# One program instead of two for the choice of experts, semaphores cleared inside the next norm, and fetches first: an eight-layer network on one core

## The reference, cut to what matters

```python
scores = softmax(xf @ gate_weight.T).T            # (8, 2048)
vals, idx = top_k(scores.reshape(-1), 2 * 2048)
gate = zeros((8, 2048)).at[idx // S, idx % S].add(vals)
h = gelu(einsum('sd,edf->esf', xf, W1) + b1[:, None, :])
y = einsum('esf,efd->esd', h, W2) + b2[:, None, :]
out = einsum('es,esd->sd', gate, y) + gelu(xf @ Ws1 + bs1) @ Ws2 + bs2
```

## Time and profile before

| | |
|---|---|
| median of 3 runs | 1896.82 us (1896.57 to 1897.28) |
| the profiled execution's own time | 1899.36 us |
| its span in the profile | 1897.6 us |
| PE busy | 1541.0 us (81%) |
| DVE busy | 1039.2 us (55%) |
| ACT busy | 924.2 us (49%) |
| POOL busy | 411.2 us (22%) |
| granted clock of PE, mean | 0.903 of full speed |

### The profile page before, as it was taken

The page is one execution under the profiler, slowest core; times in us unless marked ns, Lnnn a source line. Parts: engine busy times, 40 slices in busy tenths (PEclk is TensorE's granted clock), DMA queues, the critical chain, the costliest instruction groups (busy, mean ns, idle before and its releaser), DMA issues. The chain is left out here.

```text
span 1897.6 us, 22237 instructions
## 1 busy us (share of the span) xinstructions
PE 1541.0 (81%) x7296; PEld 664.5 (35%) x7296; DVE 1039.2 (55%) x2156; ACT 924.2 (49%) x1578; POOL 411.2 (22%) x370
## 2 busy tenths in 40 slices
PE   4699998899848898779799870674899977699997
PEld 1244443343302333234233430672122223344443
DVE  8577772100006999947577649423888825433332
ACT  4766665432257887520166640222477762234343
POOL 4101100000027898700022200560121100000000
PEclk7799998999958999989799985796699997899999
DMA  5112200100000000000111091013121102000000
GB/s 141 43 33 54 60 19 7 56 0 0 19 9 1 5 5 5 1 30 1 35 29 40 1 361 46 18 21 126 59 69 60 35 21 85 6 1 0 0 0 22
DMA packets 51965, 72.21 MB, mean 38 GB/s; under 512 B 11442, under 2 KB 44490, under 8 KB 50103
## 3 DMA queue, kind: packets, MB, share of 16 engines
q1 hardware_dynamic: 49814, 69.20, 12.0%
q0 software_dynamic: 2048, 1.73, 0.5%
HBM read 48.29 MB, written 18.12 MB: 35 GB/s over the span
## 5 line engine op out<-in xcount | busy, mean ns | idle before, releaser
L656 ACT ACTIVATE a_probs_sb<-a_t_ps 128x512 f32<-128x512 f32 x512 | 286.7, 596 | 129.3 <-PE a_t_ps L537 72.8
L747 DVE CUSTOM_DVE_ANT_0 a_biased<-a_s_ps,a_bias 128x512 f32<-128x512 f32 x256 | 166.2, 686 | 67.8 <-issue 67.6
L533 PE MATMUL a_t_ps<-a_stack 126*128 126x512 bf16 (+1 forms) x512 | 169.6, 395 | 30.4 <-DMA a_stack<-a_least_parts 11.7
L514 PE MATMUL a_s_ps<-a_stack 96*128 96x512 bf16 (+1 forms) x512 | 155.4, 412 | 39.4 <-DMA a_stack<-a_stacks 25.3
L1429 DVE TENSOR_TENSOR_SCAN s_h<-s_dA,s_dbu 128x1024 f32<-128x1024 f32 x64 | 146.6, 2290 | 52.9 <-POOL s_dbu L1394 44.3
L754 DVE TENSOR_REDUCE a_least_sb<-a_s_ps 128x2 f32<-128x1024 f32 x128 | 152.7, 1220 | 34.4 <-PE a_s_ps L514 34.1
L1394 POOL TENSOR_TENSOR s_dbu<-s_du,s_bs 128x1024 f32<-128x1024 f32 x64 | 152.3, 2391 | 29.5 <-DVE s_h L1429 27.9
L2843 ACT ACTIVATE c_hid<-c_up_ps,c_b 128x512 f32<-128x512 f32 x128 | 87.9, 687 | 143.6 <-PE c_up_ps L2812 143.6
L2853 DVE TENSOR_TENSOR c_gated_sb<-c_hid,c_g_ps 128x2048 f32<-128x2048 f32 x32 | 73.2, 2288 | 146.4 <-ACT c_hid L2843 146.4
L552 PE MATMUL a_o_ps<-a_probs_sb,a_vpad 128*16 128x512 f32 x1024 | 138.7, 615 | 0.2 <-ACT a_probs_sb L656 0.2
L2812 PE MATMUL c_up_ps<-xT,c_w 128*128 x256 | 118.0, 605 | 6.0 <-DMA c_select<-in_c_select 6.0
(11 more groups left out here) (452 smaller groups left out, 2539.9 us busy)
## 6 DMA issues: line engine op xcount, KB each, us to landing
x_wu<-in_x_wu SPq DMA_DIRECT2D x2, 4096.0 KB, 17.9
a_stacks<-a_p SPq DMA_DIRECT2D x16, 384.0 KB, 3.0
a_stack<-a_stacks SPq DMA_DIRECT2D x32, 192.0 KB, 3.9
a_stack<-a_stacks SPq DMA_DIRECT2D x64, 96.0 KB, 2.3
a_stacks<-a_p SPq DMA_DIRECT2D x16, 256.0 KB, 2.4
q_q<-q_q SPq DMA_DIRECT2D x32, 128.0 KB, 2.3
x_wd<-in_x_wd SPq DMA_DIRECT2D x2, 2048.0 KB, 33.5
c_w<-in_c_w SPq DMA_DIRECT2D x2, 2048.0 KB, 10.6
```

The lines of the kernel that those rows point to most:

```text
L514: made = nc.tensor.matmul(s_ps[:, 2 * (x % 2) + e, :], operand(0, k, pair, e, SCORE_ROWS)[:, t * P:(t + 1) * P], operand(1, k, pair, e, SC ...
L533: last = nc.tensor.matmul(out, operand(1, k, pair, e, TURNED_ROWS)[:, t * P:(t + 1) * P], operand(0, k, pair, e, TURNED_ROWS), start=True, ...
L656: nc.scalar.activation(probs[:, y % PROB_RING, e, :], bank("turned", y, e), ACT.Exp, scale=-1.0).then_inc(probs_ready, 1)
L747: nc.vector.tensor_tensor_reduce(out=biased[:, e, :], in0=s_ps[:, 2 * (x % 2) + e, :], in1=bias[:, h, at:at + N], scale=1.0, scalar=3.0e38 ...
```

## The change

- **Semaphores.** All semaphores are flags from zero. The nops that add one and their barriers are gone, and `core.sem` with them. The program that cleared a stage's semaphores is gone; POOL clears them (`clear_stale`) within the program of the next stage's norm.
- **Gated MLP.** The hardware loops are written out, with waits against constants; the order of the work is the same.
- **Layers 4 and 5** are one stage: the weights of layer 5 are loaded at the end of the prefetch of layer 4's norm, and the clearing between them is gone.
- **Sparse.** The ring of 8 fetched and 8 result tiles becomes one tile per expert. POOL issues all 32 fetches first (a fetch waits until the fourth before it has landed), then all 32 results. DVE makes places and weights for each group of 2 experts, 16 times, where it made them for 4 experts, 8 times. ACT and DVE run in a hardware loop over 8 turns of 2 groups, with six turns in the loop; PE's list stays written out. Ten of the semaphores are started at one by POOL within the routing program.
- **Choice.** `choice_route` and `choice_experts` are one program, `choice`. The loads of the two tables and of the bias go into the prefetch of the norm, in another order. PE makes the up products of unit 0 before the first count of the search. After the search PE makes one of the last four shared down products, then the places, then the other three, then the up products of units 1 and 2, the first transposes of the gates, the up products of unit 3, and from there, in each unit n, the spread of unit n+1, the up products of unit n+3 and the down products of unit n. The gelus of ACT run three units ahead in a ring of four; DVE writes the product with the gates in place. PSUM has three banks for up products of both kinds; two banks serve the routing. The loops over chunks are written out; the search stays a loop.

The diff, cut to its core ("..." marks what is left out):

```diff
-    def run_stage(self, stage, *args):
-        self.stage_sems = []
-        with ExitStack() as self.stage_ctx:
-            stage(self, *args)
-            with self.nc.Block() as block:
-                @block.gpsimd
-                def _(pool):
-                    for handle in self.stage_sems:
-                        pool.sem_clear(handle)
+    def clear_stale(self, pool):
+        for handle in self.stale_flags:
+            pool.sem_clear(handle)
+        self.stale_flags = []
+
+    def run_stages(self, stages, *args):
+        stale_ctx = ExitStack()
+        for stage in stages:
+            self.stage_ctx, self.stage_flags = ExitStack(), []
+            stage(self, *args)
+            stale_ctx.close()
+            stale_ctx, self.stale_flags = self.stage_ctx, self.stage_flags
...
 def layernorm_stage(core, xT, tag, out=None, prefetch=None, wide_range=False):
...
+        @block.gpsimd
+        def _(pool):
+            core.clear_stale(pool)
...
 def gated_mlp_stage(core, A, xT):
...
-            with pe.Fori(0, B - 1) as i:
+            for i in range(B - 1):
                 first(i)
                 up(i + 1)
                 second_and_out(i)
...
+def moe_and_query_stage(core, A, xT):
...
+                sp.dma_start(wg[:, :], A["m_wg"]).then_inc(w_loaded, 16)
+                sp.dma_start(wd[:, :, :], A["m_wd"]).then_inc(w_loaded, 16)
+                query.load(sp, A)
...
 def sparse_experts(...):
...
             def fetch(e):
-                if e >= X_RING:
-                    pool.wait_ge(turned, (e - X_RING) // PAIR + 1)
-                    pool.wait_ge(weighed, (e - X_RING) // SOME + 1)
+                if e >= SOME:
+                    pool.wait_ge(fetched[e % SOME], 16 * (e // SOME))
...
-            for e in range(X_RING):
+            for e in range(E):
                 fetch(e)
             for e in range(E):
-                if e + X_RING < E:
-                    fetch(e + X_RING)
                 scatter(e)
...
-def choice_route(core, xT, M, wr, tri, ones, ones_b, bits, unit, loaded, shared_loaded):
+def choice(core, xT, W, loaded, shared_loaded, first_loaded, w_loaded, out):
...
             last.then_inc(logits_ready, 1)
+            wait(pe, first_loaded, 32)
+            up(0)
+            wait(pe, shared_loaded, 48)
+            for i in range(B):
+                for m in range(CH_HT):
+                    count_all(CH_HT * i + m)
+                    shared_up(i, m)
+                    if i > 0:
+                        shared_down(i - 1, m)
             count_all(SEARCH_STEPS)
-            for m in range(CH_HT):
-                down(B - 1, m)
-            pe.wait_ge(equal_ready, START + 1)
+            shared_down(B - 1, 0)
+            wait(pe, equal_ready, 1)
             for n, summed in enumerate((tri, ones)):
                 last = nc.tensor.matmul(places_ps[:, n, :, :], ...)
             last.then_inc(places_ready, 1)
...
+            for m in range(1, CH_HT):
+                shared_down(B - 1, m)
+            wait(pe, w_loaded, 64)
+            for n in range(1, AHEAD):
+                up(n)
+            turn_gates(0)
+            up(AHEAD)
+            spread_gates(0)
+            turn_gates(1)
+            turn_gates(2)
+            for n in range(UNITS):
+                if n + 1 < UNITS:
+                    spread_gates(n + 1)
+                if n > 0 and n + AHEAD < UNITS:
+                    up(n + AHEAD)
+                if n == 1:
+                    turn_gates(3)
+                down(n)
...
+            def gate(n):
+                mine = hid[:, n % HID_RING, :, :]
+                wait(dve, spread_ready, n + 1)
+                wait(dve, gelu_ready, CH_HT * (n + 1))
+                nc.vector.tensor_tensor(mine, mine, g_ps[n % 2][:, :]..., ALU.mult).then_inc(gated_ready, 1)
```

More of the change, by code:

```diff
@@ L1015, in _ @@
             gate(0)
-            with dve.Fori(0, B - 1) as i:
+            for i in range(B - 1):
                 gate(i + 1)
@@ L1947, in sparse_stage @@
     results_zeroed = core.flag("x_results_zeroed")
+    counted = [core.flag(name) for name in COUNTED]
     with ExitStack() as mem:
@@ new lines, in experts @@
+            def experts(i):
+                for u in range(UNITS):
+                    up(i, u)
+                    if u == 0:
+                        turn(i, 1)
+                    if u == PAIR + 1 and not (isinstance(i, int) and i == TURNS - 1):
+                        turn(i + 1, 0)
+                    if u > 0:
+                        down(i, u - 1)
+                    elif not (isinstance(i, int) and i == 0):
+                        down(i - 1, UNITS - 1)
+            turn(0, 0)
@@ L2413, in _ @@
+            pe.wait_ge(w_loaded, 16 * 8)
+            for i in range(TURNS):
+                experts(i)
+            down(TURNS - 1, UNITS - 1)
             for i in range(B):
@@ L2490, in _ @@
+            keep(0, 0)
+            run(dve, experts)
             for i in range(B):
@@ new lines, in down @@
+            def down(n):
+                i, e = divmod(n, E)
+                wait(pe, gated_ready, n + 1)
+                if n == 0:
+                    wait(pe, y_copied, B)
+                if e == 0:
+                    wait(pe, added, i)
+                for k in range(CH_HT):
+                    last = nc.tensor.matmul(y_ps[:, :], w2[:, e, k, :], hid[:, n % HID_RING, k, :],
+                                            start=(e == 0 and k == 0), stop=(e == E - 1 and k == CH_HT - 1))
+                    if e == 0 and k == 0:
+                        nc.tensor.matmul(y_ps[:, :], b2[:, :], gates[:, cols(i)], start=False, stop=False)
+                last.then_inc(down_ready, 1)
@@ L3069, in network @@
         core.load_more_x = load_more_x
-        zeroed = core.sem("ident_zeroed")
+        zeroed = core.flag("ident_zeroed")
         with core.block() as block:
```

805 lines of the change are left out of this document (394 added, 411 removed).

## The result

The changed kernel takes 1826.98 us (median of 4 runs, 1825.61 to 1828.27) against 1897.05 (1896.57 to 1897.42): a ratio of 0.963, with an interval of 0.961 to 0.965. The forecast was 1842.8 with a range of 1834 to 1853. The sign was right and the gain too small: 72.8 us between the two spans (1897.6 and 1824.8), where 54.0 were forecast. By the medians it is 70.1 us: the profiled execution of the kernel before lies over its median, that of the changed kernel (1826.66 us) at it.

The account below looks back on a forecast made before the run. PE, busy for 1541 of 1897.6 us, was taken as the bound, so gains come from its idle or slow-clock stretches. Terms 29.9 + 0 + 4.3 + 17.3 + 2.5 = 54.0 us off 1896.8 gave 1842.8, range 1834 to 1853.

Parts of the forecast that it names:

- 1. Clearing: Entrances to programs: clearing of semaphores leaves the path, PE waits less; 29.9 us gain, bounds 26 and 31.
- Rival A: Entrances cost what they do for reasons other than clearing; if half of 23.3 us stays, 1854.5; chance 0.05.
- 2. Gated MLP: Gated MLP and layer 4: loops written out in the same order, and the prefetch, gain 0; bounds -1 and +1.
- 3. Fetches: Sparse experts: all fetches first, POOL remains the bound; 4.3 us gain, bounds 0 and 5.
- 4. Layer 8: Experts start while gates are made: 20.2 less a 1.4 wait and 1.5 for the search, 17.3 us; bounds 12 and 20.
- the head of the search: Layer 8: moving unit 0's up products before the first count delays the search, price 1.5 us.
- C: Layer 8's overlap pays half: search waits cost 6.4 us, DVE-bound sparse stage 3 us more; 1852; chance 0.12.
- D: Slower: PE is starved of instructions in layer 8's written-out units; 1908; chance 0.03.
- 5. The clock: Norms before layers 4, 8 and the last keep more clock after shorter waits; 2.5 us gain, bounds 0 and 11.
- The interpolation between two norms: Norms before layers 4 (clock 0.77) and 8 (0.86) set the gains: 1.1, 0.7 and 0.7 us for three norms.
- Rival B: Every norm keeps the full clock: six norms give 11.2 us instead of 2.5; 1834; chance 0.10.

Follow-up runs that it names:

- e4: Changed kernel with a stage's flags cleared in a program of their own again, without the nops and barriers of before: 1858.00 us, ratio 0.977.
- e1: Kernel before with the gated MLP's three loops written out and nothing else: 1890.04 us, ratio 0.996.
- e2: Kernel before, loops kept, with one line loading the silu table right after gelu1 in each turn: 1894.93 us, ratio 0.998.
- e7: Changed kernel with PE waiting for the gates before the up products of units 1 and 2: 1865.31 us, where the kernel before took 1917.47.
- e6: Changed kernel with the up products of unit 0 behind the search instead of before its first count: 1831.13 us against 1827.44 beside it.
- r_before: Kernel before, run again on a further chip: 1898.84 us.
- r_after: Changed kernel, measured again on a further chip: 1827.44 us (4 runs).
- r_after2: Changed kernel, measured again on another further chip: 1828.02 us (one run).
- e10: Changed kernel with the gated MLP's silu and gelu tables loaded ahead of the waits: 1862.36 us on a chip where the kernel before took 1917.47.
- e3: Kernel before with added, unused PE products in each clearing program, entrances as long as they were: 1879.90 us, ratio 0.991.
- e11: Changed kernel with 137 unused products where PE waits near a norm: 1852.63 us on a chip where the kernel before took 1917.47.
- e12: e11 and e10 in one: 1818.06 us, where the changed kernel beside it took 1827.44; ratio to the kernel before 0.958.

## Why the prediction was right or wrong, point by point

**1. Clearing.** Right: of the 29.9 us forecast 28.9 are waits of PE at entrances, and the column "entrance" adds up to the same 28.9. e4 shows the same from the other side (20.7 measured for a forecast of 21.6). Rival A falls.

**2. Gated MLP: the failed term.** "I take 0, bounds -1 and +1." It was 3.84 us (e1, e2). The prediction asked what a loop costs on PE's waits. It didn't ask where ACT's table loads stand. The row was in the trace of before: a load of 1.28 us with a wait for PE ahead of it in each turn, on the engine that PE waits for (`L932 <- DVE`, behind the silu). The sentence from the Trainium skill (Runtime: NRT & Kernel Launch, instruction fetch mechanics) would have given the sign by a different mechanism; the runs leave it at most the 0.20 us a turn between e1 and e2.

**3. Fetches.** Right: 5.0 measured, 4.3 forecast, the bound still POOL.

**4. Layer 8.** Right: the stretch from the last shared downs to the last product lost 19.0 us (forecast 20.2 less the wait of 1.4, 18.8), the head of the search cost 1.0 net (1.5 forecast). e7 shows in its row that the overlap pays; for the moved ups e6 has the sign, and some 2 us by the reading given there. Rivals C and D fall: the search took 40.2 us after 40.9, and the last units take 7.03 us for their sixteen products, as before.

**5. The clock: the term that was mis-sized.** 2.5 us forecast, about 12.6 measured, by the table and the first products: norms of layers 2, 4, 6, 7 and the last 1.6, 2.5, 0.9, 0.4 and 1.5; the first products of the gated MLP 1.45 (15.4 us from the first up product to the first gelu1 before, 13.9 after), of layer 4 2.0 (its logits; 7.4 us less 5.6 for the entrance leaves 1.8 to 2.0), of layer 6's routing 0.7, and the logits of layer 8 1.75 (6.91 and 5.16), less 0.2 for its norm.

These are differences of single traces. The traces of r_before, r_after and r_after2 repeat the norms within 0.4 us, so the 12.6 belong to this pair of kernels; but not each item is owed to its shorter entrance, as e1 has the 1.4 of the norm of layer 2 and the 1.5 of the first up products with the entrance as before, and the logits of layer 8 took 6.97 us again in e6, e7 and e10, behind the short entrance. Shown by runs are the sign and the order of size (e3, e11, e12).

Two steps failed. The interpolation between two norms let the clock rise a little with a shorter wait. It didn't follow the wait so smoothly: the norm before layer 4 went from 0.77 to 1.00, and that before layer 8 stayed at 0.85 for 0.86, though its wait fell by 3.5 us. And the term ended with the norm, though a clock lost in a norm is also missing in the products behind it: about 6 of the 12.6 us. The norms of layers 2, 6 and 7, for which the prediction took none, gave 2.9.

Rival B (1834, every norm at the full clock) came nearest, and for part of the right reason only: the norms of layers 6, 7 and 8 still take 11.7, 12.5 and 11.7 us, and only e11 and e12, with products in the waits, have all three at 10.2 (two of the three fell to it by chance in e10). The Trainium skill (TensorE: Matmul & The Clock Gate, part 1) has idleness lower the clock and sustained activity give it back; by that rule the traces of e3 and e12 agree.

**The sum.** 18.8 us were missing: 10.1 of clock, 3.8 of table loads, 0.7 each for the fetches and for layer 8, and 3.4 in several places of which layer 3 has the most (1.7) and that no run explains. The range failed too: the bounds of part 5 were given as 0 to 11 and those of part 2 as ±1, and the range was then cut as if part 5 could not come out at its far end together with anything else. Uncut it would still have missed by a little: all upper bounds together (31, 1, 5, 20 and 11) are 68 us, a median of 1828.8, and both of these parts came out above their own bounds (3.8 and 12.6).

## What to carry to other kernels

Price an entrance twice: its length, and the clock that PE loses in it, which is paid in the norm and in the first products behind it. On this kernel the second came out anywhere between a tenth and a half of the first (about 2 to 11 us beside 20.7, in the runs of e4). Where a wait can't be removed, small products into a bank that nobody reads can keep the clock up: some 18 us in the kernel before, 9 on top of the change. No single norm of a single trace tells whether they did. Look for table loads that stand behind a wait, and move those whose activations another engine waits for: of the loads moved in e2 and e10, those before silus paid 1.1 to 1.3 us each and those before gelu2 nothing.

## What the runs showed of the hardware that was not expected

- The granted clock in a stretch isn't a function of the code ahead of it alone: five runs of e4 on one chip lie 9 us apart in two groups, and the logits of layer 8 took 5.16 or 6.97 us behind the same code. The runs of the kernel before lay 6 to 7 us apart where there were most of them (17 and 9), those of the changed kernel under 3.
- A table load takes 1.28 us, and the silu starts 1.29 us after the load's start with nothing between them. The Trainium skill (ScalarE: Activation LUTs, What ACT_TABLE_LOAD costs) has the same 1.28 and adds a drain of 1.38; no row here shows that drain.
- A row of ACT with idleness of 13 and 19 us "remote", on one chip and only at the start of a hardware loop beside 32 queued indirect DMAs, each ended by a late rise of a semaphore that PE raises; the kernel before was 19 us slower on that chip as well. The cause is open.
